# The second channel mix moved into the first forward part, the second Gram matrix beside the first mix

## The reference

```
# layer 0, attention over channels
att = einsum('bcn,bdn->bcd', q, q)                 # Gram matrix over 65536 pixels
att = softmax(max(att) - att);  x = gamma * (att @ q) + x
# layer 1, long convolution with generated separable filters, plus x * bias
x = irfft2(rfft2(x) * rfft2(k)) + x * bias
# layer 2, 2-D Haar transform, per pixel scale v, 64x64 channel product, soft threshold tau, twice, summed,
#          inverse Haar transform, plus x
# layer 3, a second long convolution like layer 1
```

## Time and profile before

| | |
|---|---|
| median of 3 runs | 6031.75 us (6027.64 to 6034.47) |
| the profiled execution | 6024.16 us, span 6022.3 us |
| TensorE busy | 5710.0 us, 95% of the span |
| VectorE, ScalarE, GpSimd busy | 65%, 63%, 42% |
| DMA | 1216.97 MB, 202 GB/s over the span |
| mean granted TensorE clock | 0.968 of full speed |

### The profile page before, as it was taken

How to read it: one execution, slowest core, us unless ns; L and a number is a source line. 1 busy time by engine, 2 the same in 40 slices (tenths; PEclk the granted TensorE clock), 3 DMA queues, 4 the chain that set the end, 5 groups by cost and what they waited for, 6 DMA issues and landing times.

```text
span 6022.3 us, 154233 instructions
## 1 busy us (share of the span) xinstructions
PE 5710.0 (95%) x47200; PEld 4861.0 (81%) x47200; DVE 3918.0 (65%) x6260; ACT 3794.7 (63%) x6105; POOL 2526.9 (42%) x2436
## 2 busy tenths in 40 slices
PE   5897899999999999999999999999999999998689
PEld 3683788888888888888888888888888888897479
DVE  1241687557865678657775577756776578866866
ACT  1333676657766677666775577665776567756855
POOL 0000565225642366324552255423553246634942
PEclk7896999999999999999999999999999999999889
DMA  8778665766657666676666766576666755444234
GB/s 290 240 227 272 205 212 187 244 213 210 212 189 253 202 209 212 202 244 198 210 205 220 226 205 210 184 252 207 213 211 199 249 173 182 158 130 129 73 91 129
DMA packets 770795, 1216.97 MB, mean 202 GB/s; under 512 B 78854, under 2 KB 475047, under 8 KB 770568
## 3 DMA queue, kind: packets, MB, share of 16 engines
q1 hardware_dynamic: 623112, 945.61, 51.7%
q10 hardware_dynamic: 147456, 268.50, 11.8%
HBM read 808.07 MB, written 405.73 MB: 202 GB/s over the span
## 4 chain that ended last, share of the span: by engine, by line
PE 88%; DMA 3%; ACT 2%; DVE 2%; issue 2%; SPq 1%; POOL 1%; ACTq 1%; DVEq 0%; POOLq 0%
PE ps L478 29%; PE ps L480 15%; PE ps L528 9%; PE ps L496 9%; PE ps L504 8%; PE ps L488 7%; PE ps L456 4%; PE ps L538 4%; PE ps L644 3%; DMA mixed<-x 2%; DVE pix L1103 1%; ACT ps L894 1%; DMA mixed<-mid 1%; ACT x L845 1%; DVE ps L1116 0%
## 5 line engine op out<-in xcount | busy, mean ns | idle before, releaser
L1135 POOL TENSOR_TENSOR mag<-mag,sgn 128x512 f32<-128x512 f32 x896 | 1038.8, 1160 | 1815.4 <-ACT mag L764 1815.4
L1152 POOL TENSOR_TENSOR split_a<-field,split_a 128x512 fp32r<-128x512 f32 x512 | 651.0, 1271 | 1635.8 <-ACT split_a L825 1635.8
L478 PE MATMUL ps<-tab_a,img 128*128 128x256 f32 x4096 | 1237.2, 384 | 15.7 <-issue 14.7
L478 PE MATMUL ps<-tab_b,mid 128*128 128x256 f32 x4096 | 1224.6, 381 | 4.4 <-ACT mid L777 4.4
L997 DVE TENSOR_TENSOR held<-ps,v_t 128x1024 f32<-128x1024 f32 x448 | 548.5, 1224 | 619.2 <-PE ps L528 618.8
L480 PEld LDWEIGHTS ps<-tab_a,img 128*128 128x128 f32 x4096 | 782.8, 191 | 107.6
L480 PEld LDWEIGHTS ps<-tab_b,mid 128*128 128x128 f32 x4096 | 778.6, 190 | 105.0
L480 PE MATMUL ps<-tab_a,img 128*128 128x128 f32 x4096 | 790.1, 275 | 0.0
L480 PE MATMUL ps<-tab_b,mid 128*128 128x128 f32 x4096 | 787.0, 274 | 0.0
L758 ACT ACTIVATE sgn<-held 128x1024 bf16<-128x1024 f32 x448 | 473.3, 1056 | 456.5 <-DVE res L1008 454.3
L478 PEld LDWEIGHTS ps<-tab_a,img 128*128 128x128 f32 x4096 | 664.6, 192 | 73.6 <-issue 16.9
(11 more groups left out here) (97 smaller groups left out, 9090.2 us busy)
## 6 DMA issues: line engine op xcount, KB each, us to landing
img<-mixed SPq DMA_DIRECT2D x512, 256.0 KB, 3.2
tab_a<-filt SPq DMA_DIRECT2D x1024, 128.0 KB, 2.8
tab_b<-filt SPq DMA_DIRECT2D x1024, 128.0 KB, 3.0
out<-res SPq DMA_DIRECT2D x512, 256.0 KB, 3.1
coef<-res ACTq DMA_DIRECT2D x496, 256.0 KB, 3.5
pix<-in_x_pix SPq DMA_DIRECT2D x240, 512.0 KB, 4.7
mixed<-x ACTq DMA_DIRECT2D x448, 256.0 KB, 3.5
pix<-in_x_rows SPq DMA_DIRECT2D x128, 512.0 KB, 5.2
```

The source lines that it names most:

```text
L478: nc.tensor.matmul(o_ps, src[:, 0, H * half:H * half + H], tab[:, N - 1::-1], start=True, stop=False)
L1135: nc.gpsimd.tensor_tensor(mag[:, s], mag[:, s], sgn[:, s], ALU.mult).then_inc(c_mult, 1)
L1152: nc.gpsimd.tensor_tensor(split_a[:, 1], src, split_a[:, 0].bitcast(F32), ALU.subtract)\
```

## The change

The call inverse_stage(-1), which was the mix of image 1 alone, is gone. The mix of image 1 is done in forward_stage(-1): at each odd step TensorE does one mix chunk where it did a Gram chunk, and ScalarE at the end of each odd step copies and stores its two pieces, into a second array `mixed_1` and through four staging buffers of its own. The Gram chunks of image 1 move into inverse_stage(-2): after each mix chunk of image 0 comes one Gram chunk of image 1, into PSUM bank 3, from two pixel buffers. The softmax of image 1 follows at the end of that stage. At the end of forward_stage(-1) SyncE waits for the stores of `mixed_1`, loads channels 0 and 1 of image 1, waits for all coefficients of image 0, loads channels 2 and 3 and only then the first two chunks of `coef`. (Before, the two `coef` loads stood ahead of the four channels, after the second mix.)

The core of the diff ("..." marks what is left out):

```diff
     inverse_stage(-2, inv=False, mix=True)
-    forward_stage(-1, fwd=True, shrink=False, gram=True)
-    inverse_stage(-1, inv=False, mix=True)
+    forward_stage(-1, fwd=True, shrink=False, gram=False)
     for b in range(B - 2):
...
+        mixed_1 = nc.dram_tensor("mixed_1", (4, C, H // 4, 2 * N), F32, kind="Internal").ap()
...
+        staged_1 = [diff[:, 0], diff[:, 1], rows[:, 0:512], rows[:, 512:1024]]
...
+                    if b < 0 and j % 2 and not (isinstance(q, int) and q == 0):
+                        sp.wait_ge(mix_mm, 64 + 4 * q + j - 3 + CR)
+                        sp.nop(nofuse=True)
+                        load_xrows(1, 2 * q + j // 2, j // 2)
...
+                if b < 0:
+                    for s in mixed_out:
+                        sp.wait_ge(s, 16 * 32 + 16)
+                        sp.nop(nofuse=True)
+                    sp.wait_ge(f_mm2, 64 + CR)
+                    sp.wait_ge(f_x1, 64 + CR)
+                    sp.nop(nofuse=True)
+                    for j in range(4):
+                        if j == 2:
+                            for s in coef_out:
+                                sp.wait_ge(s, 16 * 32 + 16)
+                                sp.nop(nofuse=True)
+                        load_img(1, j, j)
+                        fwd_tables(j, j)
+                    load_coef(0, 0, 0)
+                    load_coef(0, 1, 1)
...
                         load_xrows(g, buf, buf)
+                    if not inv:
+                        for buf in range(2):
+                            load_pix(1, buf, buf + 2)
...
                                 load_xrows(b + 2, 8 * r + 4 + i, i % 4)
+                            if at == j and not inv and not (isinstance(r, int) and i >= 6):
+                                load_pix(1, 8 * r + 2 + i, 2 + i % 2)
                 inverse_rounds(sp, 4, inv, mix, step)
                 if not inv:
+                    sp.wait_ge(filters_out, 16 * SHIFTS)
+                    sp.nop(nofuse=True)
+                    for j in range(4):
+                        fwd_tables(j, j)
                     for s in mixed_out:
-                        sp.wait_ge(s, 16 * 16 * (b + 3) + 16)
+                        sp.wait_ge(s, 16 * 16 + 16)
                         sp.nop(nofuse=True)
-                    if b == -2:
-                        sp.wait_ge(filters_out, 16 * SHIFTS)
-                        sp.nop(nofuse=True)
-                    else:
-                        sp.wait_ge(f_mm2, 64 + CR)
-                        sp.wait_ge(f_x1, 64 + CR)
-                        sp.nop(nofuse=True)
-                    if b == -1:
-                        for s in coef_out:
-                            sp.wait_ge(s, 16 * 32 + 16)
-                            sp.nop(nofuse=True)
-                        load_coef(0, 0, 0)
-                        load_coef(0, 1, 1)
                     for j in range(4):
-                        load_img(j, j)
-                        fwd_tables(j, j)
+                        load_img(0, j, j)
+                    for buf in range(2):
+                        load_xrows(1, buf, buf)
...
+                    def mix_next():
+                        pe.wait_ge(xrows_in[j // 2], 16 * (CHUNKS // 4 + q) + 16)
+                        pe.wait_ge(mix_w_ready, 2)
+                        pe.wait_ge(mix_copied, 64 + 4 * q + 2 * (j // 2) - 2 + CR)
+                        pe.nop(nofuse=True)
+                        for half in range(2):
+                            for s in range(2):
+                                mm = nc.tensor.matmul(ps[C * half:C * half + C, 4 + 2 * (j // 2) + s, :],
+                                                      mix_w[C * s:C * s + C, :],
+                                                      xrows[j // 2][C * s:C * s + C, 512 * half:512 * half + 512],
+                                                      start=True, stop=True)
+                                if half:
+                                    mm.then_inc(mix_mm, 1)
                     opening = isinstance(q, int) and q == 0 and j < 2
+                    if b < 0 and on[0] and j % 2:
+                        mix_next()
...
                     att_turn(g)
+                    gram_edge(True, 3)
...
                             mix_four(m // 2)
+                            if not inv:
+                                gram_part(GCH // 4 + 4 * r + m // 4, 2 + m // 2 % 2, 0, GP, True, 3)\
+                                    .then_inc(gram_chunk, 1)
...
                 inverse_rounds(pe, 3, inv, mix, step)
+                if not inv:
+                    gram_edge(False, 3).then_inc(gram_done, 1)
+                    pe.wait_ge(mix_copied, 64 + CR)
+                    att_sum(1)
+                    att_turn(1)
...
+                    def mix_hand_over(s):
+                        t, at = 2 * (j // 2) + s, 2 * q + j // 2
+                        act.wait_ge(mix_mm, 64 + 2 * at + s + 1 + CR)
+                        act.wait_ge(mixed_out[t], 16 * (CHUNKS // 2 + q) + 16)
+                        nc.scalar.activation(staged_1[t], ps[:, 4 + t, :], ACT.Copy).then_inc(mix_copied, 1)
+                        act.wait_ge(mix_copied, 64 + 2 * at + s + 1 + CR)
+                        act.nop(nofuse=True)
+                        rows_of = mixed_1[2 * s:2 * s + 2].rearrange("g c t n -> (g c) (t n)")
+                        act.dma_start(rows_of[:, bass.ds(512 * at, 512)], staged_1[t]).then_inc(mixed_out[t], 16)
...
                         store()
+                    if b < 0 and on[0] and j % 2:
+                        for s in range(2):
+                            mix_hand_over(s)
                 quads(act, 16, 4 if fwd else 0, step)
...
                 inverse_rounds(act, 3, inv, mix, step)
+                if not inv:
+                    att_exp(1)
             def last_shrink(b):
...
                     att_place(g)
+                    for s in mixed_out[0:2]:
+                        dve.wait_ge(s, 16 * 16 + 16)
+                    dve.nop(nofuse=True)
+                    att_copy(1)
+                    att_rev(1)
+                    att_weights(1)
+                    att_place(1)
```

More of the change, by code:

```diff
@@ L277, in load_xrows, with load_img @@
                 sp.dma_start(xrows[buf], src).then_inc(xrows_in[buf], 16)
-            def load_img(c, d):
-                of_c = mixed[:, bass.ds(c, 1), :, :]
+            def load_img(g, c, d):
+                of_c = (mixed_1 if g == 1 else mixed)[:, bass.ds(c, 1), :, :]
                 per_c = H // 4 * 2 * N
@@ L308, in forward_stage @@
             def forward_stage(b, fwd, shrink, gram):
-                if gram and b <= 0:
+                if b == 0:
                     for buf in range(2):
@@ L387, in step @@
                             sp.nop(nofuse=True)
-                            load_img(j - 8, j - 8)
+                            load_img(b + 2, j - 8, j - 8)
                             fwd_tables(j - 8, j - 8)
@@ L444, in _, with gram_edge, gram_part @@
             pe.wait_ge(consts_in, 16 * 21)
-            def gram_edge(start):
-                return nc.tensor.matmul(ps[:, 7, 0:2 * C], zero[:, :], zero[:, :],
+            def gram_edge(start, bank=7):
+                return nc.tensor.matmul(ps[:, bank, 0:2 * C], zero[:, :], zero[:, :],
                                         start=start, stop=not start, skip_group_check=True)
-            def gram_part(uses, buf, j0, count, first):
+            def gram_part(uses, buf, j0, count, first, bank=7):
                 if first:
@@ L455, in gram_part @@
                         own = pixels[buf][:, j, C * e:C * e + C]
-                        mm = nc.tensor.matmul(ps[C * e:C * e + C, 7, 0:C], own, own,
+                        mm = nc.tensor.matmul(ps[C * e:C * e + C, bank, 0:C], own, own,
                                               start=False, stop=False, skip_group_check=True)
@@ L549, in forward_stage @@
                 f0 = 64 * (b + 1)
[L550 removed]
+                pe.wait_ge(mix_copied, 64 * (b + 2) + CR)
                 pe.nop(nofuse=True)
@@ L635, in mix_four @@
                     def mix_four(chunk):
-                        pe.wait_ge(xrows_in[chunk % 4], 16 * (8 * g + 2 * r + chunk // 4) + 16)
+                        before = 8 * g + (8 if chunk % 4 < 2 else -8) if inv else 0
+                        pe.wait_ge(xrows_in[chunk % 4], 16 * (before + 2 * r + chunk // 4) + 16)
                         pe.wait_ge(mix_w_ready, g + 1)
@@ L944, in att_copy @@
                 for e in range(2):
-                    ins = nc.vector.tensor_copy(att_s[C * e:C * e + C, :], ps[C * e:C * e + C, 7, 0:C])
+                    ins = nc.vector.tensor_copy(att_s[C * e:C * e + C, :],
+                                                ps[C * e:C * e + C, 3 if g == 1 else 7, 0:C])
                 ins.then_inc(att_copied, 1)
```

5 lines of the change are left out of this document (2 added, 3 removed).

## The result

The median of four runs of the changed kernel is 5959.27 us (5954.99 to 5962.38), that of four runs of the kernel before 6030.22 us (6027.64 to 6034.47). The ratio is 0.9883, 95% interval 0.9870 to 0.9895: 71 us, or 1.2%, faster. The prediction was 5986 us, range 5964 to 6010.

The account below looks back on a forecast made before the run. It took both mixes as bound by transfers, the rest by TensorE. First mix +54.5, ramp -2, forward part -2 and +6, its end -102 make -45.5 us: from 6031.75 to 5986 us, range 5964 to 6010.

Parts of the forecast that it names:

- part 1: First mix with a Gram beside it: period 4.75 us, stage 153.3 us in place of 98.8, +54.5 us (+50 to +65).
- (e): First stage: two thirds loads raise the rate to 377 GB/s, P = 4.2, 17 us more off, 5969 us; chance 0.10.
- (c): First stage: two pixel buffers do not keep the DMA full, P = 5.5, 23 us more, 6009 us; chance 0.08.
- Part 2: Ramp of the first forward part, first `img` load to product of channel 2: 12.7 us, not 14.7; -2 us (0 to -5).
- Part 3: First forward part, mix in place of Gram: -2 us on TensorE, +6 us for late `mid` copies and stores.
- (b): First forward part: ScalarE's queue sets the step, 16 to 38 us for hand-overs and late stores, 5996 to 6018; chance 0.12.
- (d): First forward part becomes bound by transfers, steps grow by 0.71 us or more; slower, 6044 us or more; chance 0.05.
- (f): Nearly all given back: ScalarE's queue at 38 us and starved pixel buffers at 23 together, 6020 to 6044; chance 0.05.
- Part 4: End of first forward part to first channel product: second mix and softmax go, drain and refill stay; -102 us (-98 to -106).

Follow-up runs that it names:

- b_deep: Kernel before with eight staging buffers and semaphores in place of four for the two mixes that stand alone; 5996.05 us.
- b_two: Kernel before with two staging buffers in place of four for the two mixes that stand alone; 6106.47 us.
- b_again: Kernel before, unchanged, run and profiled once more; 6028.63 us.
- a_pix4: Changed kernel with four pixel buffers in place of two for the Gram of image 1; 5960.31 us.
- a_split: Changed kernel with the second of each pair of ScalarE's hand-overs moved into the next step, behind the `mid` copy; 5954.40 us.
- a_coef1st: Changed kernel with the first two `coef` loads issued ahead of the loads of channels 2 and 3; 5948.65 us.

## Why the prediction was wrong

**The step that failed is the price of part 1.** "At 343 GB/s that is 3.06 us and 4.59 us": it took a rate at a DMA share of 0.99 for what the engines can give, and with it set the lower end of the period at 4.59. The stretch was held to that rate by four staging buffers. `b_deep` and `b_two` show it: with the transfers and their sizes the same, eight buffers give 399 GB/s and two 231. In the changed kernel the engines gave 411 GB/s, 1.573 MB a period are then 3.83 us (measured 3.82), and the stage cost +27.4 us, not +54.5 (+24.2 between `b_again` and `a_again`).

The agreement of 3.06 us with the measured 2.98 was taken as support. It was none: the period and the rate are one measurement, since bytes per period divided by the period is the rate. The trace of before gave reason to doubt. A store took 5.0 us to land, and there were four buffers; the earlier trace rows name `ACT mid` as the releaser of the last mix, and in the list of waits from 110 to 170 us ScalarE's copies waited for landings of `mixed` 22 times, 25 us in all. These waits alone don't tell the cases apart, since they stand in the changed kernel too, where the engines are full. The rate in short slices does. Kernel before, 100 to 185 us, and changed kernel, 105 to 205 us, each in 40 slices:

```profile
GB/s 400 392 381 246 364 387 391 232 369 296 404 333 289 354 384 361 298 397 388 371 273 352 336 289 325 381 287 281 365 361 370 386 220 364 358 407 320 380 234 243
```

```profile
GB/s 411 410 410 413 412 419 401 351 376 407 419 407 411 414 415 415 414 416 410 418 415 410 420 415 410 418 415 410 422 413 410 418 415 411 418 410 414 415 417 405
```

The same engines moved 400 GB/s and more in some slices of 2.1 us and 220 to 300 in others: 343 was the mean of bursts and pauses. In the changed kernel 37 of 40 slices are at 405 and more.

The Trainium skill (Perfetto Trace Analysis, section "Identifying the Most-Contended Engine") says that occupancy misleads for the DMA, because there are 16 engines. The traces agree: a share of 0.99 at 343 GB/s, 1.04 at 399 and 1.03 at 411. A share that passes 1 is no fraction of what the engines can give.

**The clock came on top.** The prediction fed its loop formula, (landing + Gram chunk + 0.3) / 2, with 2.16 us for a Gram chunk at the low clock; at the granted 0.97 it is 1.15. At the low clock TensorE alone would need 4.15 us a period, and with the measured landing the formula gives (6.3 + 2.16 + 0.3) / 2 = 4.38: 10 to 17 us more for the stage. This is an estimate; no run held the clock down in this stage. The prediction named the rise of the clock, but priced it at 5 us, because the supposed rate stood at 4.59 right below. The formula alone, (5.6 + 2.16 + 0.3) / 2 = 4.0, was nearer than the value of 4.75, which leaned on that rate.

**The rival that came nearest is (e)**, 5969 us, with P = 4.2 and 377 GB/s. Its direction is right; its reason, that loads go faster than stores, isn't needed: `b_deep` gives 399 GB/s with half loads, as before, and there ScalarE sets the period. Whether the mix of loads and stores accounts for the step from 399 to 411 isn't shown. (The 5950 given for (e) with all other terms at their better ends is a slip: 5969 - 3 - 6 - 4 = 5956.) Rival (c), pixel buffers that leave the engines idle at P = 5.5, is out. By the port figure of 436 GB/s that the Trainium skill gives (DMA: Bandwidth & Descriptors, section "Where 436 GB/s comes from") the prediction had +17 us for the stage as an estimate; by the row of 343 it was +50 at least. The measured +27.4 lies nearer to the page, and the 414 GB/s of `a_pix4` is 0.95 of its figure. The same section says that for transfers from and to main memory a side of about 358 GB/s binds; here 399, 411 and 414 were measured, and the measurement decides. To say that the trace decided here gave the trace a question that the mean of 343 didn't answer: it showed what was moved, not what could be.

**Part 2** (-2 predicted, -0.5 measured in the first pair of traces). The steps are there; the `xrows` chunk took 6.3 us instead of 5.5. Between traces of the changed kernel the ramp varies from 13.5 to 15.6, so no more can be said.

**Part 3** (+4 predicted, +0.6). The mechanism was right to the copy: late `mid` after one of two odd steps, by 0.2 us at the product, with pairs of 9.18 and 9.46. `a_split` prices it at 4 us, where 5 + 1 stood. Without it the part is 284.9 us against 288.4 before, so the exchange of Gram for mix saves 3.5 us, or 2.2 against the 287.1 of `b_again`; the predicted 2 may well be right. DMA was 0.85 at 273 GB/s, predicted 0.87 and 280. Rivals (b), (d) and (f), in which this part grows by 16 us and more, are out: it grew by 0.6 us (1.9 to 2.0 against `b_again`).

**Part 4** (-102 predicted, -103.3). Drain, two `img` and four table loads, then the landing of `coef`; `a_coef1st` moved the load and with it the product. The gap was 11.0 us, not 14. The term came out within 1.3 us.

**What was priced at nothing.** The prediction said that no stage after 621 us would change its length, and named such a change as a sign of being wrong. In the means over 14 traces the first, third and fifth inverse parts grew by 1.3, 1.0 and 1.5 us and the second forward part by 2.0: 5.8 us. The inverse parts go through one late landing of a `mixed` store each, and that store is issued 0.3 us late by ScalarE; what ties the late issue to the long landing, and both to the change, is open. The second forward part goes with the granted clock of its first 15 us. That clock differs from one execution to the next of the same kernel (0.90 and 0.73), so how much of the 2.0 us belongs to the change, and how much is scatter, is open too; the 0.73 stands only in traces without a separate second mix.

For the first pair of traces the terms add up: the sum of -45.5 becomes -77.3 at the first channel product by -27.1 (stage 1), +1.5 (ramp), -3.4 (forward), -1.3 (end) and -1.5 (the earlier start), and +7.9 of the rest makes the -69.4 by which the two spans differ.

## What to carry to other kernels

A stretch in which the DMA share is near 1 is not yet bound by the DMA engines: count the buffers that each stream has, and look whether the engine that fills them waits for landings. That buffers times bytes over the landing time gives the measured rate is no proof, for it came out in the kernel before and in the changed one alike. Look at the rate in short slices: bursts between pauses left room here, the flat row didn't. The test is one more buffer: if the rate rises and the landing hardly does (343 to 399 GB/s here, 5.0 to 5.4 us), the depth was the bound; if the landing grows and the rate stays (6.2 to 10.1 us for 3 GB/s), the engines are full. When work is moved under a part that another engine bounds, write that engine's order out to the copy, and put what nobody waits for behind what somebody does: two such edits (`a_split`, `a_coef1st`) gave 4 and about 6 us.

## What the runs showed of the hardware that was not expected

- The core moved 411 to 414 GB/s with two thirds loads and 399 with half loads, at DMA shares of 1.03 and 1.04; at 0.99 it had moved 343.
- Rows 128 KB apart in memory and contiguous chunks of the same 512 KB load at the same rate (periods 3.80 and 3.82 us with full engines).
- The granted clock of the first mix was 0.50 with the mixes alone every 2.98 us, TensorE busy 0.64 of the time, and 0.58 with the mixes every 2.57 us, busy 0.70 (`b_deep`). With the Gram chunks between the mixes it was 0.97, with TensorE busy 0.59 of the time.
- A store that ScalarE issued 0.3 us late landed in 5.3 to 6.3 us in 21 of 24 cases, where the stores at the same places of four other traces landed in 2.9 to 3.4.
